# Transposing split logits in full tiles, and adding a row's own logit on ScalarE, in a stack of four graph layers

## The chip, the cores and the metric

The kernel runs on one core of one Trainium2 chip. The metric is the device time of one execution in microseconds; three runs of the kernel before gave a median of 2636.43 us, from 2636.19 to 2638.84 us.

## The reference, cut to what matters

Input x holds 128 graphs of 128 nodes with 256 features each; all share one 128 x 128 adjacency. Four residual layers follow each other, and each begins with relu(layernorm(x)).

```python
def _gat_heads(x, adj, W, a):
    Wh = jnp.einsum('bnf,hfo->bhno', x, W)
    f1 = jnp.einsum('bhno,ho->bhn', Wh, a[:, :O])
    f2 = jnp.einsum('bhno,ho->bhn', Wh, a[:, O:])
    e = f1[:, :, :, None] + f2[:, :, None, :]
    e = jnp.where(e > 0, e, LEAKY_ALPHA * e)
    e = jnp.where(adj[None, None] > 0, e, NEG_INF)
    return jnp.einsum('bhnm,bhmo->bhno', jax.nn.softmax(e, axis=-1), Wh)
...
x = x + layer0(h)   # 4-head attention, elu, 1-head attention, elu, feed-forward, layernorm
x = x + layer1(h)   # 8-head attention with q, k, v and output projection
x = x + layer2(h)   # sum over neighbours of a linear map
x = x + layer3(h)   # 1-head attention with leaky relu 0.2; output beside its projection
```

In an attention of `_gat_heads` the score of row n and neighbour m is the row's own logit f1[n] plus the neighbour's logit f2[m]. Two such attentions have one head: the second one of layer 0 (chain C in the kernel) and that of layer 3 (chain E).

## The kernel before, in words

The 128 graphs are taken in 64 pairs. The work of a pair is cut into steps, named by their chain: A (first attention of layer 0), B (its heads and the product with W_out), C (second attention, feed-forward, layernorm), D and F (layer 1: D up to q, k and v, F from the scores on), E (layers 2 and 3). A suffix .0 or .1 is the graph of the pair.

Each engine has its list of steps (`PE_ORDER`, `ACT_ORDER`, `DVE_ORDER`, `POOL_ORDER`, lines 24 to 51) with a lag behind each name. `rounds` (line 260) walks through the list once per round: in round i the entry `E_s:7` does step E_s of pair i-7. A round so holds one step of every name, each of another pair, and at any time some eight pairs are under way. An engine takes its steps strictly in the order of its list; a step waits on semaphores (`done`, `both`, `before`) for the steps that it needs, on whatever engine, so the list decides who is held up by whom. SyncE only loads and stores x, one pair at a time.

PE's matmuls come in kinds that matter here, told apart in the rows by the stationary operand's shape (rows*columns) and the type. Most have a full 128*128 stationary operand: products of high and low halves (`split_product`, L1116; `B_wh`, L1223; marked fp32 in the rows), plain fp32 products (`heads_out`, L1190), and fp32 transposes (L1107, L1183, L1245, L1347). `F_s` (L1334) works in four tiles of 32 rows, `F_o` (L1360) in four tiles of 32 columns.

The steps of the change:

- `split_in_three` (line 428, on POOL) writes a pair's four logits (two graphs, own and neighbour's) as three bf16 parts with the same sum into columns 0 to 11 of `C_f3` or `E_f3`; `F_fcopy` does the same with the 16 reciprocals of layer 1 in 48 columns of `F_f3`.
- `C_fT`, `E_fT`, `F_fT` on PE transpose them through `logits_transposed` (L1232): the stationary operand has as many columns as the tile, so 12, 12 and 48.
- `C_fTc`, `E_fTc` (L862) and `F_fTc` (L1016) on DVE copy the 12 or 48 rows out of PSUM into a bf16 tile whose other rows are zero.
- `C_s` and `E_s` on PE (`both_logits`, L1238 and L1239) build the 128 x 128 scores of each graph from two bf16 matmuls: one puts the own logit into every column, one the neighbour's into every row. `pick` is the 0/1 tile that selects the three parts.
- `C_leaky` and `E_leaky` on ACT (`leaky`, L661) apply the leaky relu to both graphs' scores at once, 256 columns in PSUM. Then follow max (`pair_max`, DVE, L889), exp with a bias and a sum (L653), the transposes `C_pT`, `E_pT` (L1245), a copy (`C_attn`, `E_attn`, L573) and the products `C_o`, `E_o`.
- `F_rT` (L1376) spreads the reciprocals with four bf16 matmuls whose stationary operand is `F_pick`; it needs `F_fTc`.
- `F_s` of pair p waits for `F_x2` of the pair before and for `A_attn` (L615, ACT) of pair p+3, as it writes into their banks.

Of the kernel before, what the change touches and what calls it, by code (L numbers as in the profile page):

```python
# [24 lines left out]
B_wh0.0:3 E_m.0:7 F_pTa.0:6 B_wh1.0:3 B_wh2.0:3 F_pTb.0:6 D_zT:5 B_wh3.0:3 E_m.1:7 C_hT:4 B_ol.1:3 D_k:5 F_pTb.1:6  # L25
E_am:7 A_s.0:2 F_pTa.1:6 C_hid:4 D_v:5 F_fT:6 F_o:6 A_wh_hi.1:2 E_zT3:7 F_rT:6 B_oh.1:3 C_ffn:4 A_pT.0:2 A_s.1:2 E_h:7
B_wh0.1:3 D_q:5 B_wh1.1:3 A_zT:1 E_fT:7 B_wh2.1:3 B_wh3.1:3 F_out:6 A_f:1 A_pT.1:2 E_s:7 B_ol.0:2 C_fT:3 F_s:5 C_s:3
E_pT:7 A_wh_lo.0:1 E_o:7 B_oh.0:2 A_wh_hi.0:1 C_pT:3 E_zT:6 A_wh_lo.1:1 C_o:3
# [4 lines left out]
C_oexp.0:3 E_mjhigh.0:6 C_oexp.1:3 F_pTca.0:5 D_high:4 B_whc.0:2 F_expb.1:5 E_mjhigh.1:6 C_hhigh:3 F_pTcb.0:5
A_whc_lo.1:1 D_kc:4 B_negl.1:2 F_pTca.1:5 F_pTcb.1:5 A_leaky.0:1 C_hidc:3 C_high:3 B_expl.1:2 A_exp.0:1 B_highl.1:2
A_whc_hi.1:1 E_hT3:6 B_negh.1:2 B_exph.1:2 F_high:5 A_leaky.1:1 E_hc:6 B_highh.1:2 A_attn.0:1 A_exp.1:1 A_high:0
B_whc.1:2 D_qc:4 A_fround:0
# [3 lines left out]
F_on:7 A_norm.0:3 B_lowl.1:4 A_z.1:2 B_hh.1:4 A_max.1:3 C_y:5 F_low:7 A_stats.0:1 C_stats.0:5 C_moments.0:5  # L40
C_stats.1:5 C_g.0:5 A_recip.1:3 A_stats.1:1 C_moments.1:5 A_low:2 E_fTc:8 A_norm.1:3 C_x1.0:5 F_x2:7 E_stats.0:7
E_stats.1:7 A_frest:2 E_max.0:8 E_moments.0:7 E_max.1:8 C_fTc:4 E_moments.1:7 C_g.1:5 F_maxa.0:6 F_maxa.1:6
A_moments.0:1 E_recip:8 A_moments.1:1 E_z.0:7 E_left.0:8 C_max.0:4 C_max.1:4 E_left.1:8 B_hl.0:3 E_z.1:7 C_x1.1:5
D_stats.0:5 C_recip:4 D_stats.1:5 F_maxb.0:6 B_lowl.0:3 E_low:7 D_moments.0:5 D_moments.1:5 B_hh.0:3 F_maxb.1:6
# [1470 lines left out]
```

## Time and profile before

| | before |
|---|---|
| median of three runs | 2636.43 us (2636.19 to 2638.84) |
| the profiled execution's own time | 2638.98 us |
| its span on the core | 2637.1 us |
| PE busy | 2550.9 us, 97% of the span |
| weight loads (PEld) busy | 2333.0 us, 88% |
| DVE busy | 2215.3 us, 84% |
| ACT busy | 2078.0 us, 79% |
| POOL busy | 1298.0 us, 49% |
| share of PE in the chain that ended last | 93% |

A matmul's row shows when it starts and how long it takes from start to end; matmuls overlap, so what one costs is the distance from its start to the next one's start, not its duration. PEld is the load of a stationary operand, which may run while the matmul before is still streaming.

### The profile page before, as it was taken

How to read it: one execution, taken by the hardware profiler on the slowest of the kernel's cores; microseconds unless marked ns; L12 is line 12 of the kernel's file. 1: busy time of each engine (PE TensorE's matmuls, PEld its weight loads, DVE VectorE, ACT ScalarE, POOL GpSimd, SP SyncE). 2: the span in 40 equal slices, each digit the busy share in tenths (PEclk: the TensorE clock that was granted, in tenths of full speed). 3: DMA queues.
4: the chain of work that ended last, by engine and by line, in shares of the span. 5: the costliest groups of instructions: out<-in, count | busy, mean ns of one | idle time of the engine just before them, and what ended most of it. 6: DMA issues, size and time to landing. Idle time of an engine off the chain costs nothing.

```text
span 2637.1 us, 64646 instructions
## 1 busy us (share of the span) xinstructions
PE 2550.9 (97%) x21825; PEld 2333.0 (88%) x21825; DVE 2215.3 (84%) x8352; ACT 2078.0 (79%) x5708; POOL 1298.0 (49%) x2276
## 2 busy tenths in 40 slices
PE   4899999999999999999999999999999999999985
PEld 3789999999999999999999999999999999999874
DVE  5688888888888888888888888888888888888874
ACT  3788888888888888888888888888888888888852
POOL 4545455455455455455455455455545545545431
PEclk8999999999999999999999999999999999999996
DMA  4000000000000000000000000000000000000000
GB/s 129 5 2 9 18 18 10 18 17 10 17 18 14 14 17 18 10 18 18 9 18 17 10 18 18 10 18 17 10 17 18 10 18 18 12 15 14 9 9 13
DMA packets 41288, 44.32 MB, mean 17 GB/s; under 512 B 2816, under 2 KB 40448, under 8 KB 40832
## 3 DMA queue, kind: packets, MB, share of 16 engines
q1 hardware_dynamic: 40816, 39.14, 4.7%
q8 instruction: 176, 2.88, 0.5%
q14 instruction: 152, 1.25, 0.2%
q10 hardware_dynamic: 144, 1.05, 0.1%
HBM read 23.40 MB, written 16.78 MB: 15 GB/s over the span
## 4 chain that ended last, share of the span: by engine, by line
PE 93%; DVE 2%; ACT 0%; issue 0%; POOL 0%; DVEq 0%; ACTq 0%; POOLq 0%
PE pA L1116 15%; PE pB L1223 14%; PE pB L1116 10%; PE pB L1190 9%; PE pE L1116 7%; PE pC L1116 7%; PE pF L1347 4%; PE pF L1116 3%; PE pF L1360 2%; PE pE L1425 2%; PE pA L1334 2%; PE pE L1107 2%; PE pA L1183 2%; PE pC L1269 2%; PE pE L1410 1%; PE pE L1448 1%
## 5 line engine op out<-in xcount | busy, mean ns | idle before, releaser
L1223 PE MATMUL pB<-wout_high,B_h_high 128*128 128x258 f32 x1024 | 324.4, 317 | 1.5 <-POOL B_h_low L490 0.8
L704 ACT ACTIVATE F_s_t<-F_s_t,F_m 128x128 f32<-128x128 f32 x1024 | 324.7, 393 | 0.0
L1223 PE MATMUL pB<-wout_high,B_h_low 128*128 128x258 f32 x1024 | 290.4, 284 | 0.0
L1223 PE MATMUL pB<-wout_low,B_h_high 128*128 128x258 f32 x1024 | 289.7, 283 | 0.0
L1190 PE MATMUL pB<-probs,whs 128*128 128x128 f32 x2048 | 278.3, 279 | 1.8 <-DVE F_m L889 0.7
L1190 PEld LDWEIGHTS pB<-probs,whs 128*128 128x128 f32 x2048 | 250.2, 192 | 4.2 <-issue 3.7
L1116 PE MATMUL pA<-wh_high,A_hT_high 128*128 128x512 f32 x512 | 225.7, 441 | 5.3 <-POOL wh_low L398 5.3
L606 ACT ACTIVATE probs<-probs,A_m 128x128 f32<-128x128 f32 x512 | 199.4, 397 | 26.9 <-DVE A_m L889 26.9
L442 POOL TENSOR_TENSOR E_f<-E_h_t,F_zeros 128x4 bf16<-128x4 f32 x64 | 12.9, 202 | 408.4 <-ACT E_h_t L726 408.4
L1116 PE MATMUL pA<-wh_low,A_hT_high 128*128 128x512 f32 x512 | 203.6, 398 | 0.0
L1223 PEld LDWEIGHTS pB<-wout_high,B_h_high 128*128 128x128 f32 x1024 | 195.1, 190 | 8.8 <-POOL B_h_low L490 1.8
L1116 PE MATMUL pA<-wh_high,A_hT_low 128*128 128x512 f32 x512 | 202.6, 396 | 0.0
L519 POOL TENSOR_TENSOR xs<-xs,bl_b 128x512 f32<-128x512 f32 x64 | 92.6, 1447 | 214.6 <-DVE E_z_t L854 214.6
L1223 PEld LDWEIGHTS pB<-wout_low,B_h_high 128*128 128x128 f32 x1024 | 195.1, 191 | 1.9
L1223 PEld LDWEIGHTS pB<-wout_high,B_h_low 128*128 128x128 f32 x1024 | 193.9, 189 | 0.0
L915 DVE SCALAR_TENSOR_TENSOR B_e<-B_e,pB 128x512 f32<-128x512 f32 x256 | 172.9, 675 | 21.8 <-ACT B_e L632 21.7
L490 POOL TENSOR_TENSOR B_h_low<-B_e,B_h_high 128x512 fp32r<-128x512 f32 x128 | 165.3, 1291 | 48.9 <-ACT B_h_high L640 48.9
L640 ACT ACTIVATE B_h_high<-B_e 128x512 fp32r<-128x512 f32 x256 | 159.7, 624 | 33.9 <-DVE B_e L915 33.9
L1001 DVE TENSOR_REDUCE F_sum<-F_s_t 128x4 f32<-128x512 f32 x256 | 167.9, 675 | 0.6 <-ACT F_s_t L704 0.5
L632 ACT ACTIVATE B_e<-B_e 128x512 f32<-128x512 f32 x256 | 160.3, 626 | 2.0
L713 ACT ACTIVATE F_pT<-pF 128x512 f32<-128x512 f32 x256 | 145.9, 596 | 18.4 <-PE pF L1347 18.4
L854 DVE TENSOR_SCALAR E_z_t<-xs,E_mv,E_rs 128x256 f32<-128x256 f32 x256 | 97.8, 403 | 70.0 <-POOL E_rs L425 70.0
(270 smaller groups left out, 9946.4 us busy)
## 6 DMA issues: line engine op xcount, KB each, us to landing
xs<-in_x SPq DMA_DIRECT2D x64, 256.0 KB, 2.7
out_x<-xs SPq DMA_DIRECT2D x64, 256.0 KB, 2.1
probs<-in_a_heads ACTq DMA_DIRECT2D x1, 1024.0 KB, 5.1
F_pT<-in_w_heads SPq DMA_DIRECT2D x2, 512.0 KB, 6.9
xs<-in_w_out SPq DMA_DIRECT2D x1, 1024.0 KB, 9.6
...
```

The lines of the kernel that those rows point to most:

```text
L490: pool.tensor_tensor(B_hl_t[1][:, cols], B_e[:, cols], B_hl_t[0][:, cols].bitcast(F32), ALU.subtract)\
L606: last = act.activation(A_l[:, s, h, :], A_l[:, s, h, :], ACT.Exp, scale=-1.0, bias=A_m[:, s, h:h + 1], accum_out=A_sum[:, s, h:h + 1])
L632: act.activation(B_e[:, cols], B_e[:, cols], ACT.Exp, scale=-1.0).then_inc(S["B_exp" + part], 1)
L640: act.activation(B_hl_t[0][:, cols], B_e[:, cols], ACT.Copy).then_inc(S["B_high" + part], 1)
L704: last = act.activation(F_s_t[:, s, h, :], F_s_t[:, s, h, :], ACT.Exp, scale=-1.0, bias=F_m[:, s, h:h + 1])
L713: act.activation(F_pT[:, s, c * HPC:(c + 1) * HPC, :].rearrange("p h n -> p (h n)"), pF[:, c, :], ACT.Copy)\
L915: dve.scalar_tensor_tensor(out=e, in0=e, scalar=-1.0, in1=pB[:, bank, :], op0=ALU.add, op1=ALU.max)\
L1001: dve.tensor_reduce(total, e, AX.X, ALU.add).then_inc(S["F_sum" + part], 1)
L1116: last = pe.matmul(dst, a, b, start=(i == 0), stop=(i == len(terms) - 1))
L1190: last = pe.matmul(pB[:, bank, (k % 4) * P:(k % 4 + 1) * P], whs[:, s, h, c * P:(c + 1) * P], attnT[:, s, h, :], start=True, stop=True)
L1223: last = pe.matmul(pB[:, 0, 0:D + 2], a, w[:, k, :], start=(k == 0 and i == 0), stop=(k == KH - 1 and i == 2))
L1347: last = pe.transpose(pF[:, c, j * P:(j + 1) * P], F_s_t[:, s, c * HPC + j, :], ident[:, :])
```

## The change

Five things are changed.

1. `C_f3`, `E_f3` and `F_f3` become 128 x 128 tiles, zeroed once at the start (three more clears on POOL); the split writes the same columns as before, and the three transposes take all 128 columns.
2. `C_s` and `E_s` make only the neighbours' part: one bf16 matmul per graph in place of two.
3. `C_leaky` and `E_leaky` become two activations of 128 columns, each with the own logit of its graph as a per-partition bias (`wh2[:, s, D]`, `E_h_t[:, s, F3]`, fp32, as they stand).
4. `pick` keeps only the two neighbours' selections (256 columns instead of 512).
5. The four lists are new. All lags in PE's list and most in ACT's and DVE's are shifted by a whole round, which changes nothing by itself; what changes is the order within a round.

PE's lists, both begun at the same place (lags left out):

```
before: B_oh.0 A_wh_hi.0 C_pT E_zT A_wh_lo.1 C_o B_wh0.0 E_m.0 F_pTa.0 B_wh1.0 B_wh2.0 F_pTb.0 D_zT B_wh3.0 E_m.1
        C_hT B_ol.1 D_k F_pTb.1 E_am A_s.0 F_pTa.1 C_hid D_v F_fT F_o A_wh_hi.1 E_zT3 F_rT B_oh.1 C_ffn A_pT.0 A_s.1
        E_h B_wh0.1 D_q B_wh1.1 A_zT E_fT B_wh2.1 B_wh3.1 F_out A_f A_pT.1 E_s B_ol.0 C_fT F_s C_s E_pT A_wh_lo.0 E_o
after:  B_oh.0 A_wh_hi.0 E_zT C_pT A_wh_lo.1 B_wh0.0 E_m.0 F_pTa.0 F_pTb.0 C_o B_wh1.0 B_wh2.0 E_m.1 B_wh3.0 D_zT
        F_pTb.1 B_ol.1 E_am F_pTa.1 D_k A_s.0 C_hT F_fT F_o F_rT D_v E_zT3 C_hid E_h B_oh.1 A_wh_hi.1 F_out B_wh0.1
        A_s.1 A_pT.0 C_ffn D_q A_zT E_fT B_wh1.1 B_wh2.1 B_wh3.1 A_pT.1 E_s A_f F_s C_fT B_ol.0 E_pT C_s A_wh_lo.0 E_o
```

ACT's list after has `... B_whc.1 A_attn.1 E_leaky A_fround E_exp.0 E_exp.1 E_attn C_leaky ...`, DVE's `... B_hl.1 E_moments3.1 F_fTc E_z3.0 E_z3.1 C_hlow A_max.0 F_rTc F_on ...`, and POOL's has `A_fright` ahead of the next pair's `A_rstd`.

```diff
-        pick = sb("pick", [P, H0, P], BF16)
+        pick = sb("pick", [P, G, P], BF16)
...
-        F_f3, F_frest_t = sb("F_f3", [P, 3 * G * HEADS_L1], BF16), sb("F_frest_t", [P, G * HEADS_L1])
+        F_f3, F_frest_t = sb("F_f3", [P, P], BF16), sb("F_frest_t", [P, G * HEADS_L1])
...
-            for t in (C_fT_t, E_fT_t, F_fT_t):
+            for t in (C_f3, E_f3, F_f3, C_fT_t, E_fT_t, F_fT_t):
                 pool.memset(t[:, :], 0.0).then_inc(consts_built, 1)
...
-            def leaky(chain, scores, slope):
+            def leaky(chain, scores, own, slope):
...
-                    act.activation(scores, scores, ACT.Prelu, alpha=slope).then_inc(S[chain + "_leaky"], 1)
+                    for s in range(G):
+                        one = scores[:, s * P:(s + 1) * P]
+                        last = act.activation(one, one, ACT.Prelu, bias=own[:, s, :], alpha=slope)
+                    last.then_inc(S[chain + "_leaky"], 1)
...
             def logits_transposed(dst, f3):
 
-                n = f3.shape[1]
-                return pe.transpose(dst[0:n, 0:P // 2].bitcast(BF16), f3[:, :], ident_bf[:, :])
+                return pe.transpose(dst[:, 0:P // 2].bitcast(BF16), f3[:, :], ident_bf[:, :])
...
-                    one = dst[:, s * P:(s + 1) * P]
-                    pe.matmul(one, fT[:, :], pick[:, 2 * s, :], start=True, stop=False)
-                    last = pe.matmul(one, pick[:, 2 * s + 1, :], fT[:, :], start=False, stop=True)
+                    last = pe.matmul(dst[:, s * P:(s + 1) * P], pick[:, s, :], fT[:, :], start=True, stop=True)
                 return last
```

## Rows read from the trace of the kernel before

**Rows 1.** The page, part 1: busy time of each engine over the span.

```profile
PE 2550.9 (97%) x21825; PEld 2333.0 (88%) x21825; DVE 2215.3 (84%) x8352; ACT 2078.0 (79%) x5708; POOL 1298.0 (49%) x2276
```

**Rows 2.** Windows: stretch, length, busy of PE, PEld, DVE, ACT, POOL, granted clock, DMA.

```profile
0.00:100.00 100.00, 57.02 (x304) 47.63 (x305) 51.00 (x198) 49.47 (x117) 41.18 (x66) 0.92 0.28 88
400.00:2300.00 1900.00, 1900.00 (x16508) 1749.91 (x16507) 1654.44 (x6268) 1560.31 (x4309) 961.37 (x1694) 1.00 0.05 15
```

**Rows 3.** Timeline (start us, us) of PE and PEld around one E_fT, L1232.

```profile
1302.13 0.60 PE L1107 MATMUL pA<-ident,A_z_t 128*128 128x128 f32 x4
...
1302.66 0.08 PEld L1232 LDWEIGHTS pE<-ident_bf,E_f 128*12 128x12 bf16 x1 [0.17 <-issue]
...
1303.03 0.29 PE L1223 MATMUL pB<-wout_low,B_h_high 128*128 128x258 f32 x1
...
1303.15 0.29 PE L1223 MATMUL pB<-wout_high,B_h_low 128*128 128x258 f32 x1
```

**Rows 4.** Timeline of PE where no E_fT stands between the same two kinds.

```profile
1321.35 0.60 PE L1107 MATMUL pB<-ident,D_z_t 128*128 128x128 f32 x4
...
1321.91 0.29 PE L1223 MATMUL pB<-wout_low,B_h_high 128*128 128x258 f32 x1
```

**Rows 5.** Timeline of PE: B_ol.0, C_fT, then F_s.

```profile
1307.73 0.50 PE L1190 MATMUL pB<-probs,whs 128*128 128x128 f32 x3
1308.16 0.22 PE L1232 MATMUL pC<-ident_bf,C_f 128*12 128x128 bf16 x1
1308.32 0.37 PE L1334 MATMUL pA<-D_k_t,D_q_t 32*128 32x128 f32 x1
```

**Rows 6.** Timeline of PE: the end of F_s, then C_s.

```profile
1309.20 0.27 PE L1334 MATMUL pA<-D_k_t,D_q_t 32*128 32x128 f32 x1
...
1309.42 0.23 PE L1238 MATMUL pC<-pick,C_fT_t 128*128 128x128 bf16 x1
```

**Rows 7.** Timeline of PE: D_v, F_fT, then F_o.

```profile
1330.98 0.28 PE L1116 MATMUL pB<-wv_high,D_hT_low 128*128 128x256 f32 x1
1331.19 0.24 PE L1232 MATMUL pF<-ident_bf,F_f 128*48 128x128 bf16 x1
1331.36 0.64 PE L1360 MATMUL pF<-F_pT,D_v_t 128*32 128x128 f32 x16
```

**Rows 8.** Timeline of PE: the end of F_o, then A_wh_hi.1.

```profile
1332.15 0.29 PE L1360 MATMUL pF<-F_pT,D_v_t 128*32 128x128 f32 x4
1332.37 0.50 PE L1116 MATMUL pA<-wh_high,A_hT_high 128*128 128x512 f32 x1
1332.71 0.39 PE L1116 MATMUL pA<-wh_low,A_hT_high 128*128 128x512 f32 x1
```

**Rows 9.** Timeline of PE: A_pT.1, E_s, then B_ol.0.

```profile
1306.47 0.60 PE L1183 MATMUL pA<-ident,probs 128*128 128x128 f32 x4
1306.90 0.22 PE L1238 MATMUL pE<-pick,E_fT_t 128*128 128x128 bf16 x1
...
1307.07 0.22 PE L1239 MATMUL pE<-E_fT_t,pick 128*128 128x128 bf16 x1
1307.12 0.55 PE L1190 MATMUL pB<-probs,whs 128*128 128x128 f32 x3
```

**Rows 10.** Line L1232, E_fT's load: duration ns min/median/max.

```profile
L1232 PEld LDWEIGHTS pE<-ident_bf,E_f x64: 83/84/86, 203.9 to 2628.6; 128*12 128x12 bf16 x64
```

**Rows 11.** Tile E_fT_t, a full bf16 load: duration ns min/median/max.

```profile
L1238 PEld LDWEIGHTS pE<-pick,E_fT_t x128: 95/98/152, 208.0 to 2629.3; 128*128 128x128 bf16 x128
```

**Rows 12.** Groups of ACT: leaky relu, and biased exponentials; busy us, mean ns.

```profile
L704 ACT ACTIVATE F_s_t<-F_s_t,F_m 128x128 f32<-128x128 f32 x1024 | 324.7, 393 | 0.0
...
L661 ACT ACTIVATE pE<-pE 128x256 f32<-128x256 f32 x64 | 24.2, 378 | 11.2 <-PE pE L1239 11.2
```

**Rows 13.** Timeline of ACT: A_attn.1.

```profile
1307.10 0.60 ACT L615 ACTIVATE probs<-pA 128x512 f32<-128x512 f32 x1
```

**Rows 14.** Timeline of PE early on: C_s waits for a copy by DVE.

```profile
77.95 0.23 PE L1238 MATMUL pC<-pick,C_fT_t 128*128 128x128 bf16 x1 [0.31 <-DVE C_fT_t L862]
```

More of the change, by code:

```diff
@@ L24 @@
 PE_ORDER = """
[L25 to L28, printed above, removed]
+B_oh.0:2 A_wh_hi.0:1 E_zT:6 C_pT:3 A_wh_lo.1:1 B_wh0.0:2 E_m.0:6 F_pTa.0:5 F_pTb.0:5 C_o:3 B_wh1.0:2 B_wh2.0:2 E_m.1:6
@@ L29 @@
+B_wh3.0:2 D_zT:4 F_pTb.1:5 B_ol.1:2 E_am:6 F_pTa.1:5 D_k:4 A_s.0:1 C_hT:3 F_fT:5 F_o:5 F_rT:5 D_v:4 E_zT3:6 C_hid:3
+E_h:6 B_oh.1:2 A_wh_hi.1:1 F_out:5 B_wh0.1:2 A_s.1:1 A_pT.0:1 C_ffn:3 D_q:4 A_zT:0 E_fT:6 B_wh1.1:2 B_wh2.1:2
+B_wh3.1:2 A_pT.1:1 E_s:6 A_f:0 F_s:4 C_fT:2 B_ol.0:1 E_pT:6 C_s:2 A_wh_lo.0:0 E_o:6
 """.split()
 ACT_ORDER = """
-A_attn.1:2 E_leaky:7 E_exp.0:7 E_exp.1:7 B_negl.0:2 E_attn:7 C_leaky:3 B_expl.0:2 F_expa.0:5 C_exp.0:3 C_exp.1:3
-A_whc_lo.0:1 B_negh.0:2 B_highl.0:2 C_attn:3 E_high:6 B_exph.0:2 F_expa.1:5 B_highh.0:2 F_expb.0:5 A_whc_hi.0:1
@@ L33 @@
[L33 to L36, printed above, removed]
+F_pTcb.0:5 E_mjhigh.1:6 F_pTca.0:5 B_whc.0:2 D_high:4 F_pTcb.1:5 A_whc_hi.0:1 A_whc_lo.1:1 B_negl.1:2 F_pTca.1:5
+B_expl.1:2 D_kc:4 C_hhigh:3 A_leaky.0:1 B_highl.1:2 E_hT3:6 F_high:5 A_exp.0:1 C_hidc:3 C_high:3 A_whc_hi.1:1
@@ L37 @@
+B_negh.1:2 E_hc:6 B_exph.1:2 A_leaky.1:1 B_highh.1:2 A_attn.0:1 A_exp.1:1 D_qc:4 A_high:0 B_whc.1:2 A_attn.1:1
+E_leaky:6 A_fround:0 E_exp.0:6 E_exp.1:6 E_attn:6 C_leaky:2 B_negl.0:1 B_expl.0:1 C_exp.0:2 A_whc_lo.0:0 C_exp.1:2
+B_negh.0:1 B_highl.0:1 B_exph.0:1 E_high:5 F_expa.0:4 F_expb.0:4 C_attn:2 B_highh.0:1 E_mjhigh.0:5 F_expa.1:4
+C_oexp.0:2 C_oexp.1:2 F_expb.1:4
 """.split()
 DVE_ORDER = """
-E_moments3.0:8 E_stats3.1:8 E_moments3.1:8 E_z3.0:8 E_z3.1:8 A_max.0:3 F_fTc:7 D_vc:6 B_hl.1:4 F_rTc:7 A_recip.0:3
@@ L40 @@
[L40 to L44, printed above, removed]
@@ L45 @@
-F_suma.0:6 D_z.0:5 D_z.1:5 E_mjlow.0:7 C_min:4 E_mi.0:7 C_h.0:4 C_h.1:4 F_sumb.0:6 D_low:5 F_suma.1:6 F_sumb.1:6
-E_mi.1:7 E_mjlow.1:7 F_recip:6 A_z.0:1 C_hlow:4 E_x3:7 E_stats3.0:7
+A_moments.1:1 E_stats3.1:7 E_moments3.0:7 B_hl.1:3 E_moments3.1:7 F_fTc:6 E_z3.0:7 E_z3.1:7 C_hlow:4 A_max.0:2 F_rTc:6
+F_on:6 D_vc:5 F_low:6 B_lowl.1:3 A_z.0:1 A_z.1:1 A_recip.0:2 A_norm.0:2 F_x2:6 B_hh.1:3 A_max.1:2 E_stats.0:6 C_y:4
+A_stats.0:0 C_stats.0:4 C_stats.1:4 A_recip.1:2 A_norm.1:2 C_moments.0:4 C_moments.1:4 E_fTc:7 E_stats.1:6 A_low:1
@@ new lines @@
+E_moments.0:6 C_g.0:4 C_g.1:4 C_x1.0:4 C_x1.1:4 E_max.0:7 A_frest:1 E_max.1:7 E_moments.1:6 D_stats.0:4 C_fTc:3
+F_maxa.0:5 F_maxa.1:5 E_recip:7 E_z.0:6 E_z.1:6 C_max.0:3 C_max.1:3 D_moments.0:4 B_hl.0:2 E_left.0:7 E_left.1:7
+F_maxb.0:5 A_stats.1:0 B_lowl.0:2 D_stats.1:4 D_moments.1:4 E_low:6 B_hh.0:2 C_recip:3 F_maxb.1:5 F_suma.0:5
+E_mjlow.0:6 E_mi.0:6 D_z.0:4 F_suma.1:5 F_sumb.0:5 D_z.1:4 A_moments.0:0 C_min:3 C_h.0:3 F_sumb.1:5 C_h.1:3
+E_mjlow.1:6 E_mi.1:6 D_low:4 F_recip:5 E_x3:6 E_stats3.0:6
@@ L47 @@
 """.split()
 POOL_ORDER = """
-E_rstd3:7 C_low:4 E_fcopy:7 B_lowh.1:3 C_rstd:4 C_fcopy:3 C_xb:1 E_rstd:6 A_fleft:1 E_xb:6 D_rstd:4 B_lowh.0:2
-A_rstd:0 A_fright:1 C_hb:3 E_right:7 F_fcopy:5 D_xb:4
+C_rstd:5 C_fcopy:4 E_rstd:7 D_rstd:5 E_right:8 E_xb:7 B_lowh.0:3 A_fleft:2 A_fright:2 D_xb:5 C_hb:4 F_fcopy:6 A_rstd:1
+E_rstd3:7 C_low:4 E_fcopy:7 B_lowh.1:3 C_xb:1
 """.split()
@@ L160, in gnn_stack @@
         wh2 = sb("wh2", [P, G, D + 2])
-        C_f3, C_frest_t, C_fT_t = sb("C_f3", [P, 3 * 2 * G], BF16), sb("C_frest_t", [P, 2 * G]), sb("C_fT_t", [P, P], BF16)
+        C_f3, C_frest_t, C_fT_t = sb("C_f3", [P, P], BF16), sb("C_frest_t", [P, 2 * G]), sb("C_fT_t", [P, P], BF16)
         C_l, C_aT = sb("C_l", [P, G, P]), sb("C_aT", [P, G, P])
@@ L294, in gnn_stack @@
         LOADED = 16 * len(loads)
-        ZEROED = 12
+        ZEROED = 15
         BUILT = ZEROED + 11
@@ L376, in _ @@
                 pool.affine_select(out=pick[:, :, :], in_=pick[:, :, :], compare_op=ALU.not_equal, fill=1.0,
-                                   base=-part * H0, pattern=[[-1, H0], [0, P]], channel_multiplier=1)\
+                                   base=-part * 2 * G - 1, pattern=[[-2, G], [0, P]], channel_multiplier=1)\
                     .then_inc(consts_built, 1)
@@ L738, in _ @@
                 **pair("B_highl", B_high("l", LOW)), **pair("B_highh", B_high("h", HIGH)), **pair("B_whc", of_graph(B_whc)),
-                "C_leaky": leaky("C", pC[:, 0:W], SLOPE_L0), **pair("C_exp", exp_and_sum("C", C_l, C_m, C_sum)),
+                "C_leaky": leaky("C", pC[:, 0:W], wh2[:, :, D:D + 1], SLOPE_L0), **pair("C_exp", exp_and_sum("C", C_l, C_m, C_sum)),
                 "C_attn": copy("C_pT", "C_attn", C_aT[:, :, :].rearrange("p g n -> p (g n)"), pC[:, W:2 * W]),
@@ L748, in _ @@
                 "E_hT3": copy("E_zT3", "E_hT3", E_h3T[:, :], pE[:, :], ACT.Relu), "E_hc": E_hc,
-                "E_leaky": leaky("E", pE[:, 0:W], SLOPE_L3), **pair("E_exp", exp_and_sum("E", E_l, E_m_t, E_sum)),
+                "E_leaky": leaky("E", pE[:, 0:W], E_h_t[:, :, F3:F3 + 1], SLOPE_L3), **pair("E_exp", exp_and_sum("E", E_l, E_m_t, E_sum)),
                 "E_attn": copy("E_pT", "E_attn", E_aT[:, :, :].rearrange("p g n -> p (g n)"), pE[:, W:2 * W]),
@@ L1257, in C_s @@
                 done(pe, "C_fTc", p)
-                both_logits(pC, C_fT_t).then_inc(S["C_s"], 1)
+                neighbours_logits(pC, C_fT_t).then_inc(S["C_s"], 1)
             def C_pT(p):
@@ L1436, in E_s @@
                 done(pe, "E_fTc", p)
-                both_logits(pE, E_fT_t).then_inc(S["E_s"], 1)
+                neighbours_logits(pE, E_fT_t).then_inc(S["E_s"], 1)
             def E_pT(p):
```

4 lines of the change are left out of this document (2 added, 2 removed).

## The prediction

> **What bounds the kernel now.** I read the busy times first: PE has 97% of the span and the next engine 84% [rows 1]. An average over the span does not say whether PE ever waits, so the windows come second: from 400 to 2300 us PE is busy for all 1900 us at the full granted clock, while DVE has 1654 and ACT 1560 [rows 2]. In that stretch PE has no wait that another engine ends. PE's own work sets the round, then, and every other engine has slack. PE issues 21825/64 = 341 matmuls per pair, so 16508 of them in 1900 us [rows 2] are 48.4 rounds of 39.25 us. At the start it is otherwise: 57 us busy in the first 100.
>
> The timeline comes third, because a busy PE is not a PE at its peak. What a matmul costs is the distance to the next start. Within a kind these are steady: 0.11 us between fp32 transposes or fp32 products (three products [rows 5] take 0.50, of which the last takes 0.275, so two steps are 0.225), 0.12 between split products [rows 3], and (1307.07 - 1306.90)/3 = 0.056 between bf16 matmuls with full 128*128 operands [rows 9]. Around the transposes of the logits they are not. The last fp32 transpose ahead of E_fT starts at 1302.13 + 0.33 = 1302.46, E_fT's load at 1302.66 after the load path stood idle for 0.17 us, and the second product behind it at 1303.03: 0.57 us [rows 3]. Where no E_fT stands between, the same way takes 1321.91 - 1321.68 = 0.23 [rows 4]. E_fT so costs 0.34 us, six times a full bf16 matmul. The reader is to see that this is no wait for data: the idle time before the load is put down to "issue".
>
> My reading is a **boundary**: a load is not drawn ahead when the shape of the stationary operand changes (128 columns to 12, to 48, to the 32-wide tiles of F_s and F_o, and back). Each boundary costs about 0.09 to 0.11 us: C_fT starts 0.20 after the last product instead of 0.11, F_s 0.16 after C_fT instead of 0.056 [rows 5]; C_s 0.22 after the last tiles of F_s, again instead of 0.11 [rows 6]; F_fT 0.21 instead of 0.12, F_o 0.17 instead of 0.056 [rows 7]; A_wh_hi.1 0.22 instead of 0.11 [rows 8]. Where an fp32 load follows a boundary, another 0.10 shows before the second matmul (1303.03 is 0.22 after the first one's start; at A_wh_hi.1 0.34 instead of the 0.23 that twice as many columns take [rows 8]).
>
> **The change, part by part**, in us per round on PE.
>
> - *The own logits leave PE.* Four bf16 matmuls fewer: 4 x 0.056 = 0.22 [rows 9].
> - *E_fT in a full tile.* Both its boundaries go: 0.34 - 0.056 = 0.29 saved, and what every full bf16 matmul costs the fp32 load behind it comes back: three products behind E_s take 0.55 [rows 9], three in a stream 0.50 [rows 5], so 0.05. Net 0.24.
> - *C_fT in a full tile, now behind F_s.* Before, three boundaries stood in a row (into C_fT, into F_s, out of F_s). After, only those of F_s are left, and C_fT takes over the one that C_s paid [rows 6]. Saved 0.09, given back 0.05 for the load of B_ol.0. Net 0.04.
> - *C_s moves between E_pT and A_wh_lo.0*: the load behind it belongs to a split product instead of a transpose. 0.04 lost.
> - *F_fT in a full tile.* The boundary into it goes, the one into F_o stays: 0.09 saved [rows 7].
> - *F_rT moves right behind F_o.* The boundary is now paid in front of a bf16 load, without the extra 0.10 of an fp32 one: 0.09 saved [rows 8].
> - Everything else in PE's list is only reordered between kinds that show no cost between them: 0.
>
> The sum is 0.22 + 0.24 + 0.04 - 0.04 + 0.09 + 0.09 = 0.64 us per round. Some two of the 64 rounds' worth lies in filling and draining, where PE waits anyway: 62 x 0.64 = 39.7 us.
>
> Off PE: *two biased activations* of 128 columns for one of 256. One took 0.378; a biased one of 128 costs 324.7/1024 = 0.317 in a stream [rows 12], so 0.25 more per leaky, 0.5 per round. ACT's 1560/48.4 = 32.2 becomes 32.7 of a 38.6 us round: covered. Without cover, in the drain, it is 0.25 per step, against 0.24 that E_fT saves there. *Three more clears and a smaller pick* touch only POOL's first 8 us, and PE's first long job waits for weights that come later: 0. *POOL's and DVE's steps* are the same in number; DVE's 34.2 of 38.6 still has slack.
>
> *The new order in the filling.* PE idles 43 us in the first 100 [rows 2], and no row of before shows the new order there. A_s.1 now stands ahead of A_pT.0, which helps the first rounds; A_fright ahead of the next A_rstd may help or hurt. I bound it at 5 us either way, a ninth of that idle time, and take 0, since both directions occur.
>
> The profiled execution took 2639.0 us, 2.5 above the median. 2639.0 - 39.7 = 2599.3, and from the median 2636.4 - 39.7 = **2596.7 us**.
>
> **Two handoffs that the new lists tighten.** F_rT needs F_fT's copy. A transpose's end, DVE's copy and the next start lie 0.31 apart when DVE is free [rows 14]; with F_fT's own 0.24 that is 0.55 from F_fT's start. F_rT's turn comes after F_o: 0.17 + 8 x 0.11 + 0.11 = 1.16. Margin 0.6, and the copy now stands ahead of E_z3 and A_max.0. F_s needs A_attn.1, and now only E_s and A_f stand between A_pT.1 and it. From the last transpose of A_pT.1 (1306.47 + 0.33 = 1306.80) A_attn.1 ends at 1307.70 [rows 13], 0.90 later. F_s's turn comes 0.11 + 2 x 0.056 + 0.05 + 6 x 0.12 + 0.09 = 1.08 later. Less some 0.05 of handover, the margin is about 0.1 us. If it fails by 0.1, the round loses 0.1.
>
> **The rivals.**
>
> *Partly given back.* A handoff is late by 0.1 to 0.4 us in each round: 62 x (0.64 - 0.25) = 24 us saved, some 2612 us (2606 to 2621). For it: the margin at F_s. Against: A_attn.1 stands ahead of E_leaky in ACT's list. Chance 0.14.
>
> *The narrow transposes are not the cause.* The gap could belong to the transposition of a small bf16 tile as such, and a wider one would keep it. Then only the four matmuls go, and the loads grow: full ones take 98 ns, E_fT's 84 [rows 10, 11], so twice 0.014 more. 0.22 - 0.03 = 0.19 us, 12 us in all: 2624 us. Against: E_s, full and bf16, starts 0.11 after a transpose, without a gap [rows 9]. Chance 0.09. The Trainium skill ("TensorE: Matmul & The Clock Gate", section "LDWEIGHTS (loading the stationary operand)") speaks for this rival: a load's time goes with its number of columns, 1/1.2 ns each. By that, as an estimate, padding adds 97 ns to each of two loads and 67 to the third, 0.26 us a round, and eats up the four matmuls: about 2639 us. The trace disagrees: 84 ns for 12 columns, 98 for 128.
>
> *Slower.* F_s stalls on A_attn.1 in every round for longer than the round saves. It decides from 0.1 + 0.64 = 0.74 us of delay of A_attn.1 on. B_whc.1 stands ahead of it and waits for B_wh3.1, which ends only just before A_pT.1; if ACT comes 1 us late through it, F_s stalls 0.9 and the round is 0.26 longer: 2636.4 + 62 x 0.26 = 2653 us. Against: the leaky relu and the exponentials of E come behind it in ACT's list. Chance 0.07.
>
> **How the numbers follow.** The forecast has 0.64. Its own bounds: with no 0.05 lost behind full bf16 matmuls that are alone (0.14 more) and every round counted, 64 x 0.78 = 50, and 5 gained in the filling: 2581. With half the boundaries' gain only, 62 x 0.5 = 31, and 5 lost: 2610. Another 0.06 goes to more than that being saved. The range from 2581 to 2625 holds the forecast and the first two rivals, 0.87 together; it cannot end at 2621, since the forecast and the first rival alone hold 0.78. The slower case and the 0.06 lie outside. A change of 0.2%, 5 us, is about what a measurement of this kernel can tell from none. Faster: 0.64 + 0.06 + 0.14 + 0.09 less a little for stalls near the break-even = 0.90; within 0.2%: 0.03; slower: 0.07.
>
> **What would show it.** In the profile after, the three L1232 rows have 128*128 stationary operands, start 0.11 behind a transpose and leave no load idle with "issue"; L1239 is gone and L1238 has 256 instances. The round is 38.6 us (49.2 in 1900 us), PE still busy throughout, ACT 0.5 us per round busier. A wait of F_s (L1334) for L615, or of L1376 for L1016, times 62, is the partly given back case. Idle load time before L1232 with full tiles would prove the boundary wrong. The prediction is wrong if the round saves 0.64 and the time does not follow (then filling or drain grew), or if PE waits in the middle.

## The result, and the profile after

| | before | after |
|---|---|---|
| median of the first three runs | 2636.43 us | 2606.53 us (2601.98 to 2606.67) |
| ratio of the medians, 95% interval | | 0.9878 [0.9856, 0.9901] |
| the profiled execution's own time | 2638.98 us | 2601.98 us |
| its span | 2637.1 us | 2600.1 us |
| ACT busy per round, middle of the span | 32.2 us | 1609.13/49.2 = 32.7 us |

The kernel became faster by 29.9 us in the medians and by 37.0 us between the two profiled executions. The profiled execution of after is its fastest. Two more sets of four runs, beside the kernel before on the same chip, gave 2603.69 us (ratio 0.9871 [0.9855, 0.9886]) and 2603.74 us (0.9873 [0.9856, 0.9889]), which is 33.5 us faster. The prediction was 2596.7 us with a range from 2581 to 2625.

The page's busy times after, the counterpart of [rows 1]: 256 matmuls fewer, ACT 30 us busier, POOL with three clears more.

```profile
PE 2509.9 (97%) x21569; PEld 2313.4 (89%) x21569; DVE 2204.7 (85%) x8352; ACT 2107.7 (81%) x5836; POOL 1307.7 (50%) x2279
```

The windows after, the counterpart of [rows 2]. PE rests 0.19 of the 1900 us in the middle of the span, before it was none, and the first 100 us look as before.

```profile
0.00:100.00 100.00, 58.03 (x311) 48.90 (x312) 49.58 (x208) 52.01 (x124) 43.68 (x70) 0.93 0.28 88
...
400.00:2300.00 1900.00, 1899.81 (x16586) 1764.50 (x16585) 1673.53 (x6359) 1609.13 (x4478) 981.44 (x1721) 1.00 0.05 15
```

A round is best read as the distance from one F_s to the next. Its median over the steady rounds is 39.25 us before and 38.63 us after. To see what filling and draining did, the span is cut at the third and the 61st F_s: the filling, 58 rounds, the drain. Windows of the kernel before:

```profile
0.00:209.56 209.56, 164.83 (x1190) 146.11 (x1190) 139.70 (x511) 136.70 (x351) 102.00 (x159) 0.96 0.14 43
209.56:2484.46 2274.90, 2274.90 (x19770) 2095.54 (x19769) 1977.36 (x7473) 1869.09 (x5160) 1151.13 (x2027) 1.00 0.05 15
2484.46:2637.11 152.65, 111.16 (x869) 91.31 (x868) 98.23 (x373) 72.24 (x197) 44.88 (x90) 0.82 0.03 11
```

The same three windows after:

```profile
0.00:207.41 207.41, 161.85 (x1170) 143.96 (x1170) 135.12 (x508) 136.78 (x355) 104.30 (x159) 0.97 0.14 43
207.41:2448.03 2240.62, 2239.77 (x19537) 2080.33 (x19537) 1971.44 (x7474) 1897.46 (x5278) 1157.59 (x2029) 1.00 0.05 15
2448.03:2600.11 152.08, 108.33 (x863) 89.14 (x863) 98.17 (x372) 73.46 (x206) 45.84 (x93) 0.85 0.03 11
```

The 37.0 us come from the 58 rounds (2274.90 - 2240.62 = 34.28), the filling (2.15) and the drain (0.57). Only the first of the three repeats: the other profiled executions of the changed kernel have the same 58 rounds (2240.61 and 2239.80), but 209.72 and 209.35 us of filling and 155.28 and 153.22 us of drain. Against them the ends gained nothing, and the drain lost 0.6 and 2.6 us.

Now the places. E_fT after (timeline of PE and PEld; start us, us), the counterpart of [rows 3]:

```profile
1285.03 0.60 PE L1110 MATMUL pA<-ident,A_z_t 128*128 128x128 f32 x4
...
1285.36 0.10 PEld L1234 LDWEIGHTS pE<-ident_bf,E_f 128*128 128x128 bf16 x1
...
1285.47 0.22 PE L1234 MATMUL pE<-ident_bf,E_f 128*128 128x128 bf16 x1
...
1285.49 0.36 PE L1226 MATMUL pB<-wout_high,B_h_high 128*128 128x258 f32 x1
...
1285.70 0.28 PE L1226 MATMUL pB<-wout_low,B_h_high 128*128 128x258 f32 x1
```

The last transpose starts at 1285.03 + 0.33 = 1285.36, and E_fT's load starts with it: it has no idle time in brackets any more. From there to the second product are 0.34 us, where [rows 3] have 0.57 and [rows 4], without an E_fT, 0.23. The round of [rows 3] is one of the shortest: over the 49 rounds from 400 to 2300 us the median of this way is 0.586 us before (0.575 to 0.587) and 0.342 after (0.341 to 0.342).

The stretch around F_s after (timeline of PE), the counterpart of [rows 5, 6, 9]:

```profile
1287.74 0.60 PE L1186 MATMUL pA<-ident,probs 128*128 128x128 f32 x4
1288.18 0.28 PE L1239 MATMUL pE<-E_fT_t,pick 128*128 128x128 bf16 x2
1288.26 0.36 PE L1119 MATMUL pA<-A_hT_high,wa_high 128*128 128x256 f32 x1
...
1288.93 0.28 PE L1119 MATMUL pA<-A_hT_high,wa_low 128*128 128x256 f32 x1
...
1289.14 0.37 PE L1334 MATMUL pA<-D_k_t,D_q_t 32*128 32x128 f32 x1
...
1290.25 0.23 PE L1234 MATMUL pC<-ident_bf,C_f 128*128 128x128 bf16 x1
1290.32 1.11 PE L1193 MATMUL pB<-probs,whs 128*128 128x128 f32 x8
1291.26 0.38 PE L1245 MATMUL pE<-ident,E_l 128*128 128x128 f32 x2
1291.48 0.27 PE L1239 MATMUL pC<-C_fT_t,pick 128*128 128x128 bf16 x2
1291.57 0.48 PE L1119 MATMUL pA<-wh_high,A_hT_high 128*128 128x512 f32 x1
```

Before, the same eight steps (A_f, A_pT.1, E_s, B_ol.0, C_fT, F_s, C_s and E_pT, up to the start of A_wh_lo.0) ran from the first to the second of these lines of PE's timeline:

```profile
1305.76 0.28 PE L1116 MATMUL pA<-A_hT_high,wa_high 128*128 128x256 f32 x1
...
1309.80 0.48 PE L1116 MATMUL pA<-wh_high,A_hT_high 128*128 128x512 f32 x1
```

That is 4.04 us before and 1291.57 - 1287.74 = 3.83 after (medians of 49 rounds 4.038 and 3.823). F_s keeps its two boundaries: it starts 0.21 behind the product ahead of it, where products stand 0.12 apart.

The stretch around F_o after, the counterpart of [rows 7, 8]:

```profile
1270.93 0.60 PE L1110 MATMUL pC<-ident,C_h_t 128*128 128x128 f32 x4
1271.36 0.22 PE L1234 MATMUL pF<-ident_bf,F_f 128*128 128x128 bf16 x1
1271.51 1.08 PE L1360 MATMUL pF<-F_pT,D_v_t 128*32 128x128 f32 x32
1272.53 0.40 PE L1376 MATMUL pF<-F_fT_t,F_pick 128*128 128x128 bf16 x4
1272.73 0.36 PE L1119 MATMUL pB<-wv_high,D_hT_high 128*128 128x256 f32 x1
```

F_fT now starts 0.10 behind the last transpose (1270.93 + 0.33), as E_fT does above (0.11); F_o's boundary stays (0.15).

Last the waits of PEld from 400 to 2300 us after (us in total, times, longest). What the list has left are two boundaries, into F_o and out of it, beside single waits of 0.4 us of PEld and 0.2 of PE; those of F_s, read above from the starts, do not appear in it. Neither handoff that the prediction named is there.

```profile
PEld pF L1376 <- issue: 9.7, 49, 0.2
PEld pF L1360 <- issue: 7.7, 49, 0.2
```

### The profile page after: what moved, and what is told of

Same layout as the page of the kernel before. It is cut to its first block, busy times and chain, and to the rows that moved or that the text cites. A ratio compares the mean times of both kernels' runs of the same rounds, so it can differ in the third digit from the quotient of the medians.

```text
span 2600.1 us, 64265 instructions
## 1 busy us (share of the span) xinstructions
PE 2509.9 (97%) x21569; PEld 2313.4 (89%) x21569; DVE 2204.7 (85%) x8352; ACT 2107.7 (81%) x5836; POOL 1307.7 (50%) x2279
## 4 chain that ended last, share of the span: by engine, by line
PE 92%; ACT 2%; DVE 2%; issue 2%; POOL 1%; SPq 1%; DMA 0%; DVEq 0%; ACTq 0%; POOLq 0%
PE pA L1119 15%; PE pB L1226 14%; PE pB L1119 10%; PE pB L1193 9%; PE pE L1119 7%; PE pC L1119 7%; PE pF L1347 4%; PE pF L1119 3%; PE pF L1360 2%; PE pA L1334 2%; PE pE L1110 2%; PE pE L1425 2%; PE pC L1269 2%; PE pA L1186 2%; PE pE L1410 1%
## 5 line engine op out<-in xcount | busy, mean ns | idle before, releaser
L707 ACT ACTIVATE F_s_t<-F_s_t,F_m 128x128 f32<-128x128 f32 x1024 | 318.9, 396 | 0.0
L496 POOL TENSOR_TENSOR C_hid_low<-C_hid_t,C_hid_high 128x512 fp32r<-128x512 f32 x64 | 83.5, 1304 | 452.9 <-ACT C_hid_high L573 452.9
L1226 PE MATMUL pB<-wout_high,B_h_high 128*128 128x258 f32 x1024 | 307.5, 300 | 1.7 <-DVE B_h_low L926 1.0
L423 POOL TENSOR_TENSOR D_ve<-D_mv,eps 128x2 f32<-128x2 f32 x64 | 12.6, 197 | 365.7 <-DVE D_mv L850 365.7
L482 POOL TENSOR_SCALAR A_right<-A_f_t,right_keep,right_ones 128x256 fp32r<-128x256 f32 x256 | 158.8, 632 | 0.0
L716 ACT ACTIVATE F_pT<-pF 128x512 f32<-128x512 f32 x256 | 153.8, 602 | 3.4 <-PE pF L1347 3.4
```

Of the source, the lines that this page charges most:

```text
L482: last = pool.tensor_scalar(A_right[:, :, h, :], f, right_keep[:, h:h + 1], right_ones[:, h:h + 1], ALU.mult, ALU.add)
L707: last = act.activation(F_s_t[:, s, h, :], F_s_t[:, s, h, :], ACT.Exp, scale=-1.0, bias=F_m[:, s, h:h + 1])
L716: act.activation(F_pT[:, s, c * HPC:(c + 1) * HPC, :].rearrange("p h n -> p (h n)"), pF[:, c, :], ACT.Copy)\
L1226: last = pe.matmul(pB[:, 0, 0:D + 2], a, w[:, k, :], start=(k == 0 and i == 0), stop=(k == KH - 1 and i == 2))
```

## The experiments

Each ratio is to the kernel before, run on the same chip as the experiment. "Round" is the median distance from F_s to F_s.

### Is it the narrow tile?

**pad_E**: the kernel before, with nothing changed but the width of one of the three transposes.

```diff
-        E_f3, ... = sb("E_f3", [P, 3 * 2 * G], BF16), ...
+        E_f3, ... = sb("E_f3", [P, P], BF16), ...
...
-            for t in (C_fT_t, E_fT_t, F_fT_t):
+            for t in (E_f3, C_fT_t, E_fT_t, F_fT_t):
```

> The kernel before, with only E's logits in a 128-column tile (one more clear on POOL); nothing else. Boundary theory: E_fT costs 0.11 us instead of 0.34, 0.24 us a round: 39.01 us, time 2637.1 - 62 x 0.24 = 2622.2 us; the second split product behind it comes 0.34 us after the last transpose instead of 0.57. Rival (narrowness is not the cause): 2637 us.

Measured: 2623.88 us (2623.54 to 2624.36), ratio 0.9947 [0.993, 0.9963], round 38.98 us. PE's timeline of it:

```profile
1293.31 0.60 PE L1107 MATMUL pA<-ident,A_z_t 128*128 128x128 f32 x4
1293.75 0.22 PE L1232 MATMUL pE<-ident_bf,E_f 128*128 128x128 bf16 x1
1293.78 0.37 PE L1223 MATMUL pB<-wout_high,B_h_high 128*128 128x258 f32 x1
1293.98 0.28 PE L1223 MATMUL pB<-wout_low,B_h_high 128*128 128x258 f32 x1
```

The way from the last transpose's start to the second product is 1293.98 - 1293.64 = 0.34 us, as in the changed kernel. Padding alone, with more columns to load, takes 13.5 us off the time (2637.33 to 2623.88), as expected. The rival in which the gap belongs to the transposition of a small tile as such falls. So does the rule of the Trainium skill ("TensorE: Matmul & The Clock Gate", section "LDWEIGHTS (loading the stationary operand)") as a price for this: by it the load grows with its columns, and here the load of 128 columns took 98 ns against 84 for 12, and the way got shorter.

**pad_64**: the changed kernel, with the three tiles 64 columns wide (`C_f3` and `F_f3` are edited like `E_f3`). Is it the width by degree, or only "full or not"?

```diff
-        E_f3, ... = sb("E_f3", [P, P], BF16), ...
+        E_f3, ... = sb("E_f3", [P, P // 2], BF16), ...
...
-                return pe.transpose(dst[:, 0:P // 2].bitcast(BF16), f3[:, :], ident_bf[:, :])
+                return pe.transpose(dst[0:P // 2, 0:P // 2].bitcast(BF16), f3[:, :], ident_bf[:, :])
```

> The changed kernel with 64 columns in the three tiles of split logits and reciprocals instead of 128. Boundary theory (any change in the shape of the stationary operand keeps the load from being drawn ahead): E_fT costs 0.34 us again, C_fT has its own two boundaries and F_fT one: round 38.63 + 0.36 = 38.99 us, time 2603.7 + 62 x 0.36 = 2626 us. Rival (it is a matter of degree, by the number of columns): half of that or less, under 2615 us. By the loads alone, which a row per column would set: no change or less than now.

Measured: 2635.77 us (2633.93 to 2638.25), ratio 0.9993 [0.9984, 1.0002], round 39.10 us. Half a tile is no half gain: 0.47 of the 0.61 us per round are given up, and in the time nearly the whole gain. The rival of a matter of degree falls (it had the time under 2615 us), and so does the one that goes by the loads alone. The expectation itself was too low, 38.99 us and 2626. The load's row (duration ns min/median/max), and the timeline of PE and PEld around it:

```profile
L1234 PEld LDWEIGHTS pE<-ident_bf,E_f x64: 106/106/128, 207.5 to 2626.6; 128*64 128x64 bf16 x64
```

```profile
1301.73 0.60 PE L1110 MATMUL pA<-ident,A_z_t 128*128 128x128 f32 x4
1302.25 0.11 PEld L1234 LDWEIGHTS pE<-ident_bf,E_f 128*64 128x64 bf16 x1 [0.17 <-issue]
1302.25 0.24 PE L1234 MATMUL pE<-ident_bf,E_f 128*64 128x128 bf16 x1
1302.43 0.39 PE L1226 MATMUL pB<-wout_high,B_h_high 128*128 128x258 f32 x1
1302.65 0.29 PE L1226 MATMUL pB<-wout_low,B_h_high 128*128 128x258 f32 x1
```

From 1302.06 to 1302.65 are 0.59 us, and the load path is put down as idle for "issue" again. Over the middle the median of this way is 0.598 us; with 12 columns in the same lists (lists_only, below) it is 0.574. Against the changed kernel the way from the matmul ahead of the transpose to the second one behind it grew by 0.26 us at E_fT, 0.15 at C_fT and 0.12 at F_fT. Of the 32 us of time, 27.0 lie in the 58 rounds of the profiled executions (2267.65 against 2240.62); the rest lies in the ends, which differ between executions. The load is longer than that of 12 columns (84 ns [rows 10]) and also longer than that of all 128 (98 in the changed kernel's rows). With the gap in place 64 columns were worse than 12, by 0.02 us at E_fT. The Trainium skill ("TensorE: Matmul & The Clock Gate", section "Weight-path perf modes — Fast Weight Load (FWL) and DoubleRow") says that the fast weight load is on when the number of weights is 128 and the type is not fp32. The 106 ns for 64 columns against 98 for 128 agree with that, while no run here shows which mode a load was in.

### The own logit on ScalarE

**own_only**: the kernel before with only the own logit moved (narrow transposes, old lists).

```diff
-                    act.activation(scores, scores, ACT.Prelu, alpha=slope).then_inc(S[chain + "_leaky"], 1)
...
+                        last = act.activation(one, one, ACT.Prelu, bias=own[:, s, :], alpha=slope)
...
-                    pe.matmul(one, fT[:, :], pick[:, 2 * s, :], start=True, stop=False)
-                    last = pe.matmul(one, pick[:, 2 * s + 1, :], fT[:, :], start=False, stop=True)
+                    last = pe.matmul(dst[:, s * P:(s + 1) * P], pick[:, s, :], fT[:, :], start=True, stop=True)
```

> The lists of before and the narrow tiles of before (12, 12 and 48 columns); only the own logit goes to ScalarE. Boundary theory: four bf16 matmuls of 0.056 us less per round, nothing else: round 39.25 - 0.22 = 39.03 us, time 2636.4 - 62 x 0.22 = 2622.5 us, and 26 us more than the run with all edits in the old order. Rival (narrow transposes are not the cause): the same time as that run within 3 us.

**edits_old_lists**: all edits of the change, with the four lists of before. Against the changed kernel only `PE_ORDER`, `ACT_ORDER`, `DVE_ORDER` and `POOL_ORDER` differ: they are those of the kernel before.

> All edits of the change, but the four lists of before. Boundary theory: with the old order C_fT stands between B_ol.0 and F_s, F_rT behind E_zT3; three boundaries less around E_fT and C_fT and F_fT, four matmuls less, no second 0.05 behind C_fT, but F_o again in front of an fp32 load. The sum per round is again 0.64 us, so the round is 38.6 us and the time some 2597 us, as near the changed kernel as the filling and draining let it; if the drain of the new lists is what cost 3 us in the changed kernel, this one is 2 to 4 us faster than it. Rival (the new lists are needed, since the longer leaky relu makes PE wait for E_pT in the old order): PE waits at L1245 in every round, and the time is over 2606 us.

Measured: own_only 2630.45 us (2628.74 to 2631.82), ratio 0.9974 [0.9964, 0.9984], round 39.11; edits_old_lists 2610.87 us (2610.18 to 2611.71), ratio 0.99 [0.9886, 0.9913], round 38.81. A new wait of PEld stands in the middle of the latter (400 to 2300 us):

```profile
PEld pE L1245 <- ACT E_l L653: 7.9, 49, 0.2
```

In the old PE list E_pT comes straight behind C_s, and the exponentials of E, which it transposes, come behind the leaky relu that now takes longer. The load waits 7.9/49 = 0.16 us per round there. In own_only no such wait is listed, but the timelines show it: ACT's last instruction for E's exponentials and PE's next steps.

```profile
1344.28 0.18 ACT L653 ACTIVATION_READ_ACCUMULATOR E_l<-E_l,E_m_t 128x1 f32 x1
...
1344.34 0.28 PE L1240 MATMUL pC<-C_fT_t,pick 128*128 128x128 bf16 x2
1344.51 0.44 PE L1246 MATMUL pE<-ident,E_l 128*128 128x128 f32 x2
1344.71 0.48 PE L1119 MATMUL pA<-wh_high,A_hT_high 128*128 128x512 f32 x1
```

E_pT starts 0.05 us after ACT ends (1344.28 + 0.18), and in 40 rounds of the middle this distance is 52 to 53 ns, in own_only as in edits_old_lists. C_s to A_wh_lo.0 takes 0.37 us, where before it took 1309.80 - 1309.42 = 0.38 (the first start is in [rows 6]): the two matmuls that left C_s gave nothing. tuned1 (below) has all edits and the same three steps in the same order, but gives E_pT more time; there the exponentials are done 0.60 us ahead of E_pT, and the way takes 0.26:

```profile
1329.85 0.28 PE L1239 MATMUL pC<-C_fT_t,pick 128*128 128x128 bf16 x2
1329.97 0.39 PE L1245 MATMUL pE<-ident,E_l 128*128 128x128 f32 x2
1330.11 0.48 PE L1119 MATMUL pA<-wh_high,A_hT_high 128*128 128x512 f32 x1
```

In edits_old_lists it is 0.47 (median), so being late costs PE 0.2 us per round there and 0.11 in own_only. At E_s the two matmuls that left gave 0.11. So own_only saves some 0.13 us per round instead of 0.22, and both runs gained less than the theory expected for the same reason. The rival of edits_old_lists came true: PE waits at L1245 in every round, and the time is over 2606 us. The rival of own_only did not: the two runs lie 19.6 us apart.

### The lists

**lists_only**: the kernel before with the new lists. **after_again**: the changed kernel once more.

```diff
-... E_fT B_wh2.1 B_wh3.1 F_out A_f A_pT.1 E_s B_ol.0 C_fT F_s C_s E_pT A_wh_lo.0 E_o
+... E_fT B_wh1.1 B_wh2.1 B_wh3.1 A_pT.1 E_s A_f F_s C_fT B_ol.0 E_pT C_s A_wh_lo.0 E_o
```

> The kernel before with the new lists alone. Boundary theory: F_rT behind F_o saves 0.09 us a round; the narrow C_fT behind F_s has a boundary on each side of its own beside that into F_s, with an fp32 load behind it: 0.10 lost; C_s in front of a split product 0.04 lost. Round 39.25 + 0.05 = 39.30 us, time 2636 to 2643 us. Rival (the lists carry a good part of the gain): under 2626 us.

Measured: 2640.97 us (2639.34 to 2642.81), ratio 1.0015 [1.0006, 1.0023], round 39.21, drain 155.51 us. The time is within the 2636 to 2643 expected, though the round came out 0.09 below the 39.30; the rival, under 2626 us, falls. By themselves the new lists gain 0.04 us in the median round and 0.8 us in the 58 rounds (2274.11 against 2274.90), and the drain is 2.9 us longer; the medians are 3.9 us apart, lists_only being the slower (2637.12 for the kernel before beside it).

What they are worth shows only with the edits: from edits_old_lists to the changed kernel it is 2610.87 - 2603.69 = 7.2 us of time and 38.806 - 38.633 = 0.17 us per round. That is less than two single moves give in the old lists, as tuned1 and tuned2 below show: 0.22 for the cover of E_pT and 0.12 for F_rT. Something else in the new order takes about 0.17 of it back (38.63 in the changed kernel against 38.46 in tuned2, with the same edits); of that the prediction had priced 0.09, the 0.05 behind C_fT and the 0.04 at C_s.

> The changed kernel itself, to see how its runs lie: its three runs were 2602.0, 2606.5 and 2606.7 us, and the profile (2602.0) has rounds of 38.63 us. If the 4.7 us are a matter of the single execution, ten runs lie between 2601 and 2608 us on both sides of 2604; if the first was an outlier, the median is 2606 us or more.

The repetition gave 2603.69 us (2602.44 to 2607.48) and the 38.63 us per round, within the expected range, on both sides of 2604; filling and drain are told of above.

**after_swap** and **after_third**: the drain. With the new lists PE waits there for E_zT's input ahead of C_pT, which before stood first (waits of PE in the drain of after):

```profile
PE pE L1110 <- DVE xs L1064: 6.1, 5, 2.0
```

```diff
-B_oh.0:2 A_wh_hi.0:1 E_zT:6 C_pT:3 A_wh_lo.1:1 ...
+B_oh.0:2 A_wh_hi.0:1 C_pT:3 E_zT:6 A_wh_lo.1:1 ...
```

> The changed kernel with one swap in the list of PE: C_pT ahead of E_zT, as in the old lists. Theory: in the drain, where PE has little else to do, E_zT waits for E_left and holds up C_pT behind it (some 2 us over the last rounds), and that is what the new lists cost there. Then the round stays at 38.63 us, the stretch from the 61st F_s to the end falls from 152.1 to 155.5 us (three executions with the new lists) to 150 to 152.5, and the time is 2 to 3 us below that of the changed kernel run beside it, about 2601. Rival: the loss in the drain comes from other places of the new lists; then stretch and time stay within 1.5 us of the changed kernel's. A third way: in the steady rounds E_zT behind C_pT delays what follows it on VectorE, and the round grows by over 0.03 us, 2 us in all.

> The changed kernel once more, beside the run with C_pT and E_zT swapped: 2601.5 to 2607.5 us as in its seven runs so far, rounds of 38.63 us, and 152 to 155.5 us from the 61st F_s to the end.

Measured: after_swap 2604.53 us (2603.89 to 2605.45), after_third 2603.74 us (2602.39 to 2606.6): no difference. The wait shrank from 6.4 us in after_third to 2.4, but the drain took 156.90 us instead of 153.22, at a lower granted clock. A wait that after_third does not list stands in its place (waits of PE in the drain of after_swap), now for C_pT's input:

```profile
PE pC L1245 <- ACT C_l L653: 2.9, 2, 2.1
```

My theory of the drain falls: the swap moved the wait and did not shorten the time. The drains of all executions, with the clock granted to PE there (a mean between its two levels, 1.2 and 2.4 GHz):

| lists | drain us (granted clock) |
|---|---|
| old | before 152.65 (0.82), own_only 152.77 (0.82), edits_old_lists 151.41 (0.83), pad_E 153.31 (0.83), tuned1 151.78 (0.82), tuned2 152.75 (0.82) |
| new | after 152.08 (0.85), after_third 153.22 (0.85), after_again 155.28 (0.83), lists_only 155.51 (0.83), pad_64 156.20 (0.81), after_swap 156.90 (0.79) |

The means are 152.4 us for the old lists and 154.9 for the new ones, from single executions whose ranges overlap. At a clock of 0.82 to 0.83 the new lists have 155.3 and 155.5 us, the old ones 151.4 to 153.3. The times of lists_only point the same way, 3.9 us slower with 58 rounds that are 0.8 us shorter. So the new lists seem to cost 2 to 5 us outside the steady rounds. The changed kernel's own three drains are shorter at the higher clock, 152.1 and 153.2 us at 0.85 against 155.3 at 0.83; which of the two causes the other is not shown. Which step of the new lists costs the time stays open.

### A faster version

**tuned1** keeps the old lists with all edits and takes the wait at E_pT away; **tuned2** adds the move of F_rT.

```diff
 tuned1, PE:  -... F_out A_f A_pT.1 E_s B_ol.0 ...        +... F_out A_pT.1 E_s A_f B_ol.0 ...
 tuned1, ACT: A_fround moved from the list's end to right behind E_leaky
 tuned1, DVE: A_frest moved from ahead of E_max.0 to behind E_max.1
 tuned2, PE:  -... F_fT F_o A_wh_hi.1 E_zT3 F_rT ...      +... F_fT F_o F_rT A_wh_hi.1 E_zT3 ...
 tuned2, DVE: F_fTc moved ahead of A_max.0
```

> All edits, the lists of before, and one step moved as the new lists have it: A_f stands behind E_s on PE (A_fround behind E_leaky on ACT, A_frest behind E_max.1 on DVE), so that E_pT comes 0.7 us later after E_s. Theory (in the old order PE waits some 0.16 us a round at E_pT for the exponentials behind the two slower leaky activations, and what the new lists give is that cover): the wait at L1245 goes, the round falls from 38.81 to 38.64 us, and with the old drain the time is 2610.9 - 62 x 0.165 = 2600.6 us, some 3 us under the changed kernel's 2603.7. Rival (the new lists' gain lies in many places): 2606 us or more.

> As tuned1, and F_rT right behind F_o (F_fTc on DVE ahead of A_max.0). Boundary theory: F_o is then followed by a bf16 load instead of an fp32 one, 0.09 us a round: round 38.55 us, time 2595 us. Rival (F_rT waits for DVE's copy, or the later A_max.0 delays A_pT.0): the round is 38.64 us or longer, and a wait at L1376 or L1186 shows.

Measured: tuned1 2600.76 us (2597.96 to 2601.51), ratio 0.9857 [0.9842, 0.9871], round 38.58; tuned2 2593.43 us (2592.53 to 2595.94), ratio 0.9832 [0.9818, 0.9847], round 38.46. All that PEld still waits for in the middle of tuned2:

```profile
PEld pF L1376 <- issue: 9.7, 49, 0.2
PEld pA L1334 <- issue: 7.9, 50, 0.2
```

The wait at E_pT is gone, and the round fell by 0.22 us with tuned1 (0.17 expected) and by 0.12 more with tuned2 (0.09 expected). Neither rival came true. Five moves in the old lists, aimed at two places that the traces showed, beat the four new lists: 2593.43 us is some 10 us below the changed kernel.

## Why the prediction was right

- **The bound.** PE set the round before and sets it after; the only wait for another engine listed in the middle is one of 0.2 us. The forecast's 38.6 us per round is the 38.63 measured.
- **The boundary.** E_fT was to save 0.24; by the medians it saves 0.586 - 0.342 = 0.24, in the changed kernel and in pad_E alone. pad_64 adds what the prediction did not say: the boundary is not paid by degree, and of 12, 48, 64 and 128 columns only 128 avoids it. pad_E and pad_64 do not separate a change of shape from a tile that is not full. The tiles of F_s bear on it (timeline of PEld and PE before):

```profile
1308.31 0.18 PEld L1334 LDWEIGHTS pA<-D_k_t,D_q_t 32*128 32x128 f32 x1
...
1308.42 0.18 PEld L1334 LDWEIGHTS pA<-D_k_t,D_q_t 32*128 32x128 f32 x1
...
1308.53 0.27 PE L1334 MATMUL pA<-D_k_t,D_q_t 32*128 32x128 f32 x1
```

  The first load, behind C_fT, starts 0.01 us ahead of its matmul at 1308.32 [rows 5]. The second has the same shape as the loads before it and starts 0.11 ahead of its matmul. So these loads are drawn ahead although their tiles are not full, which speaks for the change of shape. No run has two narrow bf16 tiles in a row.

  One reading of the prediction is off: it puts "another 0.10" before the second matmul down to the boundary. Without an E_fT that step is long too:

```profile
1321.71 0.36 PE L1223 MATMUL pB<-wout_high,B_h_high 128*128 128x258 f32 x1
```

  From there to the second product of [rows 4] are 0.20 us, against 0.22 behind the narrow E_fT. The 0.34 that E_fT costs is read over the whole way and does not depend on it.
- **Own logits, C_fT and C_s.** 0.22 + 0.04 - 0.04 = 0.22 was forecast for the stretch from A_f to A_wh_lo.0, 4.04 - 3.83 = 0.21 measured. own_only against tuned1 shows that 0.11 of it hangs on E_pT having its input in time.
- **F_fT, F_rT and everything only reordered.** 0.18 + 0 was forecast. What is left of the measured 39.246 - 38.633 = 0.61 is 0.61 - 0.24 - 0.21 = 0.16. That is a remainder, and its closeness is in part luck. F_fT gave 0.12: from the matmul ahead of it to F_o the median is 0.376 us before and 0.258 after. F_rT's move gave 0.12 where it was tried alone (tuned2). If it gives as much in the new lists, their other reordering lost some 0.08 us, where the prediction has 0. The term for F_rT has the right size partly for another reason than the one given: in tuned2 the first step of A_wh_hi.1 behind it still takes 0.31 us, against 0.34 in tuned1, and 0.05 comes from B_oh.1, whose first product no longer stands behind a bf16 matmul (0.11 to the second one instead of 0.17).
- **The leaky relu.** Forecast: 0.25 us more per step and ACT at 32.7 us per round, covered. ACT came to 32.7. The cover is a matter of the lists, though: in the old ones it costs 0.2 per round with all edits. The prediction put the price of missing cover in the drain alone.
- **The handoffs.** F_s's margin on A_attn.1 was put at about 0.1. In the timeline of ACT after, A_attn.1 ends at 1288.38 + 0.60 = 1288.98:

```profile
1288.38 0.60 ACT L615 ACTIVATE probs<-pA 128x512 f32<-128x512 f32 x1
```

  F_s starts at 1289.14, so 0.16 us to spare. In the drain F_s waits for it once, 0.7 us. The partly given back case and the slower one did not happen.
- **Sums and signs.** Two sums of the prediction do not come out. A handoff late by 0.1 leaves 62 x 0.54 = 33 us, so the partly given back case begins at 2603 us and not at 2606. With half of the 0.42 that the boundaries are to give, the round saves 0.43 and not 0.5, so that bound is some 2615 us and not 2610. Both stay inside the range. And C_fT could not start 0.11 behind a transpose, as the signs have it, since the new list puts it behind F_s; it starts 0.20 behind F_s's last matmuls.

What was off is the size of the total, by 3 to 10 us. The step is "some two of the 64 rounds' worth lies in filling and draining": the 39.7 us count 62 rounds. The 58 rounds between third and 61st F_s gave 34.28 us, 0.59 each on the mean, and the ends gave +2.7 us in the execution first profiled, -0.4 and -2.8 in the other two. "The new order in the filling" was put at 0, and nothing here speaks against it: 207.4, 209.4 and 209.7 us against 209.56. But only the filling got that bound; the drain, where the new lists seem to cost 2 to 5 us, got none.
